# One transformer block on one core: the start of attention with the modulation as rows, gate work moved to later slots, four moves at the seams of the MLP

## The chip, the cores and the metric

One core of a Trainium2 chip runs the whole program. TensorE (PE) multiplies matrices into PSUM banks of 512 columns; VectorE (DVE), ScalarE (ACT) and GpSimd (POOL) do the elementwise work; SyncE (SP) and ScalarE issue DMAs. The metric is the device time of one execution in microseconds. The times below are the median of three executions and one profiled execution.

## The reference

```
mod = (silu(c) @ wmod).reshape(8, 6, 1, 512)      # c: 8x512, wmod: 512x3072
sa, ca, ga, sb, cb, gb = mod[:, 0..5]
ga, gb = sign(g) * maximum(|g|, 0.25)             # each gate, sign(0) = +1
h = layernorm(x) * (1 + ca) + sa                  # x: 8x512x512
x = x + ga * attention(h, W_attn, W_proj)         # 16 heads of 32, causal
h = layernorm(x) * (1 + cb) + sb
x = x + gb * mlp(h)                               # 512-1024-1024-512, relu
```

All of it is in float32; the kernel gets there with operands split into a high and a low part of reduced precision and three products of them for each matmul (TERMS).

## The kernel before

`attention` and then `mlp` run as two stages, each with its own program for each engine and with semaphores between the engines. In `attention` the eight batches are worked in a pipeline of slots: slot p handles head pair p (of 8), and has five units u. In a unit TensorE writes scores by query (`score` banks) for pair p and scores by key (`key_score` banks) for pair p-2, the weighted values of pair p-3 (`o_bank`), and some items of the list `SEQUENCE`: four TURNs (transposes of the normalised x, then modulated into `h_parts`), eight QK units of four items, eight V units of two. Items of the next batch lie in slots 4 to 7. `WORK` and `PER_SLOT` set this order by hand; every engine walks the same slots in program order. For the first batch the items of slots 4 to 7 have nothing to lie beside, so they run ahead of slot 0 (`before_first`: four TURNs, QK 0 to 3, one V unit). The names of this part, with their lines:

- `mod_columns(s)` (PE, L769) makes shift and scale as columns (512 values down the partitions, 8 batches across): 32 matmuls of 8 moving columns for a half s of the modulation (0 for attention, 1 for the MLP). `take_columns` (DVE, L619, L620) and `take_mod` (L569) read them.
- `gate_rows(g)` (PE, L776) makes a gate as 8 rows of 512: four matmuls of 512 moving columns. `take_gate` (DVE, L627 to L636) turns it into the clamped gate in five operations and SP stores it (L350).
- `wqkv_raw` is loaded in six blocks; `weights_high(k)` (ACT, L502) and `weights_low(k)` (DVE, L613) split block k. QK 0 and QK 1 need blocks 0 and 1.
- A TURN goes from PE (L725) to ACT `modulate` (`full`, L468), DVE `h_high` (L578) and POOL `low_part` (L403); QK 0 (PE, L735) waits for the low part of each quarter. `qk_hi` (ACT, L473) and `qk_lo` (DVE, L582) take a QK unit, and `load_stack(n, g)` (SP, L322) copies it with 12 DMAs into `stack[g]`, from which slots 2g and 2g+1 make their scores.
- `ones(g)` (POOL, L388) writes two rows of ones in `stack[g]`.

In `mlp` each layer is a product by seven half-size products (Strassen's form) for each of 8 batches: chunks n = 0 to 7 expand, 8 to 15 middle, 16 to 23 contract. `product(n, s)` (PE, L2149, in the last layer L2145) waits for the low part of its data operand (`lo`, DVE, L1703) and, in the first chunk of a layer, of its weights (`w2_lo` L1841, `w3_lo` L1846). `w2_sum` (L1806, L1813) makes sums of weight blocks. `second_sum` (L1727) adds up a result and has to wait until its buffer has been stored. SP's loads and stores of this stage run through one queue in program order.

## Time and profile before

| | us |
|---|---|
| median of three executions (lowest, highest) | 1541.73 (1539.03, 1541.76) |
| profiled execution | 1542.99 |
| its span from first to last instruction | 1541.2 |

The span is 1.8 us shorter than the time of the same execution; the rest lies around it. A row of the timeline gives start, duration, engine, line, what is written and read, and in brackets how long the engine was idle before it and who ended that. In rows by stretch each engine has its busy time and the count of its instructions. A TensorE record's duration includes its way through the array, so starts tell the pace better than durations; a float32 matmul of 512 columns leaves two records.

### The profile page before, as it was taken

What the parts mean: (1) busy time and instruction counts of PE and PEld (TensorE: products, weight loads), DVE (VectorE), ACT (ScalarE), POOL (GpSimd) and SP (SyncE); (2) the same over time, 40 slices, a digit from 0 to 9 for tenths busy, and PEclk for the clock granted to TensorE, in tenths of its full rate; (3) what the DMA queues carried; (4) which work ended last, traced back from release to release, by engine and by line L of the source; (5) the groups of instructions that cost most, each with busy time, mean ns of one, the idle gap of its engine ahead of it and who ended that gap; (6) DMA issues with size and microseconds to landing.
All of it is one profiled execution on the core that took longest, in us unless ns stands there. A gap on an engine that the chain in (4) does not pass through costs nothing.

```text
span 1541.2 us, 30440 instructions
## 1 busy us (share of the span) xinstructions
PE 1449.8 (94%) x12112; PEld 1314.9 (85%) x12112; DVE 1109.9 (72%) x1957; ACT 808.2 (52%) x1462; POOL 439.2 (28%) x451
## 2 busy tenths in 40 slices
PE   7989999999999999995599999998999999999998
PEld 6678878787888888874489999998999999999998
DVE  5377877777777877673577676787766666788887
ACT  3156666667666667674355555566333333353331
POOL 2146665667666766664000000000000000000000
PEclk9889999999999999997799999999999999999999
DMA  6634435244434343442434454363765556688895
GB/s 219 164 85 102 120 84 127 72 121 96 119 82 121 83 123 93 98 98 81 172 126 162 158 176 159 138 213 135 251 234 201 201 210 215 231 295 266 296 304 184
DMA packets 126590, 247.16 MB, mean 160 GB/s; under 512 B 13672, under 2 KB 36200, under 8 KB 126448
## 3 DMA queue, kind: packets, MB, share of 16 engines
q1 hardware_dynamic: 122816, 242.57, 50.5%
q10 hardware_dynamic: 3632, 2.64, 0.5%
q8 instruction: 96, 1.57, 0.4%
q14 instruction: 46, 0.38, 0.1%
HBM read 114.58 MB, written 79.72 MB: 126 GB/s over the span
## 4 chain that ended last, share of the span: by engine, by line
PE 45%; DVE 4%; ACT 2%; DMA 1%; issue 1%; SPq 0%; DVEq 0%; ACTq 0%
PE sum_b L2149 12%; PE sum_e L2149 8%; PE sum_a L2149 8%; PE aux L2089 6%; PE sum_b L2145 4%; PE sum_e L2145 3%; PE sum_a L2145 3%; PE aux L2099 1%; PE aux L2077 1%; DVE w L1841 1%; DVE op L1703 1%; DMA wproj_whole<-wproj_t 1%; ACT u_c L1443 0%; DMA y_dram<-u_c 0%; DMA blk<-y_dram 0%
## 5 line engine op out<-in xcount | busy, mean ns | idle before, releaser
L429 POOL TENSOR_TENSOR prob_lo<-prob,prob_hi 128x512 f16<-128x512 f32 x256 | 296.9, 1165 | 140.8 <-ACT prob L533 140.5
L526 ACT ACTIVATE prob_hi<-key_score 128x512 f16<-128x512 f32 x320 | 191.1, 597 | 130.6 <-PE key_score L824 128.2
L2149 PE MATMUL sum_b<-op,w 128*128 128x256 f32 x1728 | 217.9, 284 | 3.2 <-DVE p_c L1743 1.6
L735 PE MATMUL lin<-h_parts,wqkv 128*128 128x512 f32 x768 | 218.5, 408 | 1.1 <-DVE h_parts L578 1.1
L2149 PEld LDWEIGHTS sum_b<-op,w 128*128 128x128 f32 x1728 | 211.2, 192 | 5.4 <-issue 3.3
L533 ACT ACTIVATE prob<-key_score 128x512 f32<-128x512 f32 x320 | 190.7, 596 | 0.0
L697 DVE TENSOR_REDUCE row_max<-score 128x1 f32<-128x512 f32 (+2 forms) x384 | 180.4, 499 | 12.8 <-PE score L811 12.1
L735 PEld LDWEIGHTS lin<-h_parts,wqkv 128*128 128x128 f32 x768 | 143.0, 195 | 30.5 <-DVE h_parts L578 3.2
L811 PE MATMUL score<-stack 96*128 96x512 f32 (+3 forms) x512 | 155.2, 364 | 0.0
L2149 PE MATMUL sum_e<-op,w 128*128 128x256 f32 x1152 | 146.6, 284 | 3.7 <-DVE w L1841 2.3
L2149 PE MATMUL sum_a<-op,w 128*128 128x256 f32 x1152 | 145.4, 284 | 0.9 <-issue 0.9
L2149 PEld LDWEIGHTS sum_e<-op,w 128*128 128x128 f32 x1152 | 141.6, 192 | 4.6 <-DVE w L1841 2.5
L824 PE MATMUL key_score<-stack 98*128 98x512 f32 (+3 forms) x512 | 144.1, 343 | 0.0
L2149 PEld LDWEIGHTS sum_a<-op,w 128*128 128x128 f32 x1152 | 141.1, 192 | 1.8 <-issue 1.0
L844 PEld LDWEIGHTS o_bank<-v_parts,prob_hi 128*128 128x128 f16 x1280 | 100.3, 99 | 29.1 <-issue 25.7
L844 PE MATMUL o_bank<-v_parts,prob_hi 128*128 128x97 bf16 x1280 | 117.2, 212 | 5.3 <-POOL prob_lo L429 2.5
L844 PE MATMUL o_bank<-v_parts,prob_lo 128*128 128x65 bf16 x1280 | 114.3, 196 | 0.0
L745 PE MATMUL lin<-wqkv,h_parts 128*128 128x256 f32 x768 | 108.9, 284 | 0.0
L745 PEld LDWEIGHTS lin<-wqkv,h_parts 128*128 128x128 f32 x768 | 102.3, 190 | 5.1
L844 PEld LDWEIGHTS o_bank<-v_parts,prob_lo 128*128 128x128 f16 x1280 | 101.8, 100 | 0.2
L2089 PE MATMUL aux<-wproj,turned 128*128 128x512 f32 x384 | 95.3, 403 | 2.8 <-DVE turned L1600 2.8
L795 PE MATMUL score<-mask_qk,ident_bf 128*128 128x256 bf16 (+1 forms) x320 | 82.9, 259 | 13.9 <-DVE row_max L697 7.1
(153 smaller groups left out, 2577.1 us busy)
## 6 DMA issues: line engine op xcount, KB each, us to landing
stack<-qk_parts SPq DMA_DIRECT2D x384, 128.0 KB, 2.4
late_op_whole<-y_dram SPq DMA_DIRECT2D x40, 512.0 KB, 4.9
y_dram<-u_c SPq DMA_DIRECT2D x32, 512.0 KB, 3.0
blk<-y_dram SPq DMA_DIRECT2D x32, 512.0 KB, 4.1
y_dram<-y_sum SPq DMA_DIRECT2D x24, 512.0 KB, 4.4
x_tiles<-x SPq DMA_DIRECT2D x32, 256.0 KB, 3.7
attn_dram<-o_rows SPq DMA_DIRECT2D x32, 256.0 KB, 2.3
attn_tiles<-attn_dram SPq DMA_DIRECT2D x8, 1024.0 KB, 6.1
```

The lines of the kernel that those rows point to most:

```text
L429: nc.gpsimd.tensor_tensor(prob_lo[:, key[1] % 2, u, :], prob[:, u, :], prob_hi[:, key[1] % 2, u, :], ALU.subtract).then_inc(lo_pool, 1)
L526: nc.scalar.activation(prob_hi[:, q % 2, u, :], bank[:], ACT.Exp, scale=SOFTMAX_SCALE, bias=P_SHIFT)
L533: nc.scalar.activation(prob[:, u, :], bank[:], ACT.Exp, scale=SOFTMAX_SCALE, bias=P_SHIFT)\
L697: last = nc.vector.reduce_max(row_max[:, p % 2, hh, t:t + 1], bank[:, col:col + P * (t + 1)], AX.X)
L735: mm = nc.tensor.matmul(lin_bank_of((QK, f))[:], wqkv[:, wl, c, at:at + P], h[:, hl, c, :], start=(c == 0 and k == 0), stop=(c == NC_ - 1 ...
L745: mm = nc.tensor.matmul(lin_bank_of((V, g, t))[:, 0:C // 2], h[:, hl, c, t * P:(t + 1) * P], wqkv[:, wl, c, at:at + C // 2], start=(c == 0 ...
L811: mm = nc.tensor.matmul(bank[:, col:col + n], rows[:, 0, t * P:(t + 1) * P], rows[:, 1, 0:n], start=False, stop=True, skip_group_check=True)
L824: mm = nc.tensor.matmul(bank[:, col:col + n], rows[:, 1, t * P:(t + 1) * P], rows[:, 0, t * P:T], start=False, stop=True, skip_group_check ...
L844: mm = nc.tensor.matmul(o_bank[:, i * VW + low:(i + 1) * VW], part[:, p % 2, u, at:at + P], v[:, j, head, low:VW], start=(j == 0 and part ...
L2089: mm = nc.tensor.matmul(bank[:], turned[:, dl, c, t * P:(t + 1) * P], wproj[:, wl, c, :], start=(c == 0 and i == 0), stop=(c == NC_ - 1 an ...
L2145: mm = nc.tensor.matmul(dst, data[:, dl, c, cols], w3[s][:, wl, c, :], start=begin, stop=end, skip_group_check=again)
L2149: mm = nc.tensor.matmul(dst, w[:, wl, c, cols], data[:, dl, c, :], start=begin, stop=end, skip_group_check=again)
```

## The change

At the start of attention TensorE first runs 16 matmuls of the bf16 identity with itself (`warm_up`), as soon as POOL has made it. Then shift and scale are made as rows, as the gates were (`mod_row_of`, `condition_row`: four matmuls of 512 columns each), copied out by ACT (`take_row`), and turned into columns by eight small transposes (`mod_columns`). For the MLP's half this is done in slot 0 (u 1 and 3) and slot 1 (u 4), no longer ahead of slot 0; the gates' rows are made in slot 1 (u 2) and slot 2 (u 2), and their arithmetic is four operations on DVE, one to a unit, in slots 2 and 3. The four first TURNs have four banks and four buffers for themselves; QK 0 and 1 take turns by quarters; the six weight blocks are split in another order. SP loads the MLP's modulation and the first gate right behind the weights, copies `stack0` head by head, with one semaphore for each, stores the gates in slot 3, and copies `stack3`, which now shares its place with the gates, only after that. POOL makes the ones of `stack2` in slot 1 and those of `stack3` in slot 4.

In the MLP: `load_x2(1)` moves behind the stores of chunk 16's start; `w2_sum(2)` and `w2_sum(3)` go half by half to later places; `w2_lo(6)` goes ahead of three operations of chunk 8; in chunk 16 `lo(n, 4)` goes ahead of `w3_lo(5)` and `w3_lo(6)` behind `lo(n, 5)`.

TensorE's order at the start of the program, before (`lin<-ident,x_tiles` are the TURNs, `lin<-h_parts,wqkv` the QK items, `lin<-wqkv,h_parts` the V unit):

```order
L769 MATMUL o_bank<-silu,wmod_sb 128x8 x32
L725 MATMUL lin<-ident,x_tiles 128x128 x16
L735 MATMUL lin<-h_parts,wqkv 128x512 x24
L769 MATMUL o_bank<-silu,wmod_sb 128x8 x32
L735 MATMUL lin<-h_parts,wqkv 128x512 x24
L745 MATMUL lin<-wqkv,h_parts 128x256 x12
```

and now:

```order
L843 MATMUL score<-ident_bf 128x512 x16
L848 MATMUL key_score<-wmod_sb,silu 8x512 x8
L801 MATMUL lin<-ident,x_tiles 128x128 x8
L863 MATMUL o_bank<-ident,mod_rows 128x8 x8
L801 MATMUL score<-ident,x_tiles 128x128 x8
L811 MATMUL lin<-h_parts,wqkv 128x512 x48
L821 MATMUL lin<-wqkv,h_parts 128x256 x12
```

Both runs of 32 narrow matmuls are gone; the 48 QK matmuls follow each other.

VectorE's order in slot 1, from unit 0's row maximum to unit 4's (`row_max<-score` is what frees a score bank), before:

```order
L697 TENSOR_REDUCE row_max<-score 128x1
L582 TENSOR_TENSOR qk_parts<-lin,qk_parts 128x512
L559 BN_STATS bn_stats<-x_tiles 128x6
L562 BN_AGGR mean_var<-bn_stats 128x2
L697 TENSOR_REDUCE row_max<-score 128x1 x2
L559 BN_STATS bn_stats<-x_tiles 128x6
L562 BN_AGGR mean_var<-bn_stats 128x2
L627 TENSOR_SCALAR gate_sign<-key_score 8x512
L628 COPY gates<-key_score 8x512
L630 SCALAR_TENSOR_TENSOR gates<-gates 8x512
L633 TENSOR_SCALAR gates<-gates 8x512
L636 TENSOR_TENSOR gates<-gates,gate_sign 8x512
```

The same stretch now, and below it what stands in slot 3:

```order
L773 TENSOR_REDUCE row_max<-score 128x1
L650 TENSOR_TENSOR qk_parts<-lin,qk_parts 128x512
L627 BN_STATS bn_stats<-x_tiles 128x6
L630 BN_AGGR mean_var<-bn_stats 128x2
L773 TENSOR_REDUCE row_max<-score 128x1 x2
L627 BN_STATS bn_stats<-x_tiles 128x6
L630 BN_AGGR mean_var<-bn_stats 128x2
L756 TENSOR_SCALAR max_rows<-turn 8x128
```

```order
L697 TENSOR_SCALAR gate_sign<-gates 8x512
L773 TENSOR_REDUCE row_max<-score 128x1 x2
L650 TENSOR_TENSOR qk_parts<-lin,qk_parts 128x512
L642 TENSOR_SCALAR x_tiles<-x_tiles,mean_var,rstd 128x512
L701 TENSOR_TENSOR gates<-gates,gate_sign 8x512
```

The gate operations left slot 1 and lie one by one between the row maxima of slots 2 and 3.

VectorE's order at the start of chunk 16, before (`u_c<-sum_b,p_c` is `second_sum`, `late_op` a data operand's low part):

```order
L1682 TENSOR_TENSOR y_sum<-u_c,y_sum 128x1024
L1846 TENSOR_TENSOR w_5<-w_5_whole,w_5 128x1024
L1846 TENSOR_TENSOR w_6<-w_6_whole,w_6 128x1024
L1727 TENSOR_TENSOR u_c<-sum_b,p_c 128x512
L1703 TENSOR_TENSOR late_op<-late_op_whole,late_op 128x1024
L1736 TENSOR_TENSOR u_c<-sum_e,u_c 128x512
L1703 TENSOR_TENSOR late_op<-late_op_whole,late_op 128x1024
```

and now:

```order
L1790 TENSOR_TENSOR y_sum<-u_c,y_sum 128x1024
L1811 TENSOR_TENSOR late_op<-late_op_whole,late_op 128x1024
L1954 TENSOR_TENSOR w_5<-w_5_whole,w_5 128x1024
L1835 TENSOR_TENSOR u_c<-sum_b,p_c 128x512
L1844 TENSOR_TENSOR u_c<-sum_e,u_c 128x512
L1811 TENSOR_TENSOR late_op<-late_op_whole,late_op 128x1024
L1954 TENSOR_TENSOR w_6<-w_6_whole,w_6 128x1024
```

`lo(16, 4)` stands ahead of `second_sum`, and one of the two weight parts behind the operand of the next product.

The diff, cut to what sets times and order:

```diff
-        raw = Memory(nc, raw_ctx).sb("wqkv_raw", [P, NC_, 3 * C])
-    stack += [mem.sb(f"stack{g}", [P, 2, 4, T], F32R) for g in range(GROUPS // 2, GROUPS)]
+        wm_gate = raw_mem.sb("wmod_gate", [P, NC_, C])
+    stack.append(mem.sb("stack2", [P, 2, 4, T], F32R))
     with ExitStack() as gate_ctx:
+    stack.append(mem.sb("stack3", [P, 2, 4, T], F32R))
...
+    WARM_UP = 16
...
+    def turn_bank_of(n, c):
+        return score_bank[c - 2] if n == 0 and c >= 2 else lin_bank_of((TURN, c))
...
+                if n == 0 and g == 0:
+                    sp.sem_inc(stack_in[0], 16 * STACK_DMAS)
                     for j in range(4):
-                        src = f32(qk_parts[32 * j:32 * j + 32, g % 2, :, :, :]).rearrange("p s l n -> p (s l) n")
-                        step = 2 + k_part - q_part
-                        sp.dma_start(f32(stack[g][32 * block_row:32 * block_row + 32, :, j, :]),
-                                     src[:, q_part:q_part + step + 1:step, :]).then_inc(stack_in[g], 16)
+                        for block_row in range(3):
+                            load_rows(g, block_row, j, first_stack_in[j])
+                    return
+                if n == 0 and g == 3:
+                    sp.wait_ge(gates_out, 16)
+                for block_row in range(3):
+                    for j in range(4):
+                        load_rows(g, block_row, j, stack_in[g])
...
-            for step in (1, 2):
-                sp.wait_ge(mod_mm, step)
-                for half in range(2):
-                    load_mod(sp, 2 * step + half)
-                for item in before_first():
-                    if item[0] == QK and item[1] // 2 == step - 1:
-                        after_item(0, item)
+            for half in range(2):
+                sp.wait_ge(mod_mm, half + 1)
+                load_mod(sp, 2 + half)
+            load_mod(sp, 4)
+            for item in before_first():
+                after_item(0, item)
...
-                    if first and (p, u) == (1, 3):
+                    if first and (p, u) == (3, 0):
                         sp.wait_ge(gate_step, GATE_STEPS)
...
+                if first and p == 1:
+                    pool.wait_ge(w_lo, len(W_ORDER))
+                    pool.wait_ge(v_split, values_until(1))
+                    ones(2)
+                    pool.wait_ge(ones_ready, 4)
+                if first and p == 4:
+                    pool.wait_ge(mod_mm, 6)
+                    pool.wait_ge(gates_out, 16)
+                    pool.wait_ge(v_split, values_until(4))
+                    pool.wait_ge(lo_pool, 3 * len(LO_ON_POOL))
+                    ones(3)
+                    pool.wait_ge(ones_ready, 1 + GROUPS)
...
+            def take_row(s, j):
+                act.wait_ge(mod_mm, 2 * s + j + 1)
+                nc.scalar.copy(mod_rows[:, s, j], key_bank[j][0:B, :]).then_inc(mod_row, 1)
+            def take_gate(g):
+                act.wait_ge(mod_mm, 4 + g + 1)
+                act.wait_ge(w_lo, len(W_ORDER))
+                nc.scalar.copy(gates[:, g], (key_bank[0], o_bank)[g][0:B, :]).then_inc(gate_row, 1)
+            for j in range(2):
+                take_row(0, j)
+            weights_high(0)
             for item in before_first():
                 after_item(0, item, very_first=True)
+                if item == (TURN, 1):
+                    weights_high(1)
                 if item == (TURN, NC_ - 1):
+                    weights_high(2)
+                if item == (QK, 1, NC_ - 1):
                     for k in range(3, len(W_ORDER)):
                         weights_high(k)
 
             def slot(b, p, first, more):
                 if first and p == 2:
-                    act.wait_ge(gates_out, 16)
+                    act.wait_ge(mod_turned, 2)
                 for u in range(UNITS):
+                    if first and p == 0 and u in (2, 4):
+                        take_row(1, u // 2 - 1)
+                    if first and (p, u) == (1, 2):
+                        take_gate(0)
+                        load_mod(act, 5)
+                    if first and (p, u) == (2, 3):
+                        take_gate(1)
...
+            def gate_part(g, i):
+                made = 4 * g
+                if i == 0:
+                    dve.wait_ge(gate_row, g + 1)
+                    nc.vector.tensor_scalar(sign[:, g], gates[:, g], 0.0, 0.5, ALU.is_ge, ALU.subtract)\
+                        .then_inc(gate_step, 1)
+                elif i == 1:
+                    dve.wait_ge(gate_step, made + 1)
+                    nc.vector.tensor_tensor(gates[:, g], gates[:, g], sign[:, g], ALU.mult).then_inc(gate_step, 1)
+                elif i == 2:
+                    dve.wait_ge(gate_step, made + 2)
+                    nc.vector.tensor_scalar(gates[:, g], gates[:, g], GATE_FLOOR / 2, 4.0, ALU.max, ALU.mult)\
+                        .then_inc(gate_step, 1)
+                else:
+                    dve.wait_ge(gate_step, made + 3)
+                    nc.vector.tensor_tensor(gates[:, g], gates[:, g], sign[:, g], ALU.mult).then_inc(gate_step, 1)
...
-            for k in range(3):
-                weights_low(k)
             take_columns(0)
             dve.wait_ge(mod_taken, 2)
             take_mod(0)
+            weights_low(0)
             for item in before_first():
                 after_item(0, item)
-                if item == (TURN, NC_ - 1):
-                    for k in range(3, len(W_ORDER)):
-                        weights_low(k)
-            take_columns(1)
+                if item == (TURN, 1):
+                    weights_low(1)
+                if item == (QK, 1, NC_ - 1):
+                    weights_low(2)
+            weights_low(3)
...
+                    if first and p == 0 and u in (1, 3):
+                        weights_low(4 + u // 2)
+                    if first and (p, u) == (2, 0):
+                        take_columns(1)
+                    if first and p in (2, 3) and u:
+                        gate_part(p - 2, u - 1)
...
+            def warm_up():
+                for _ in range(WARM_UP):
+                    nc.tensor.matmul(score_bank[0][:], ident_bf[:], ident_bf[:].unsqueeze(1).broadcast_to([P, NT, P]),
+                                     start=True, stop=True)
+            def condition_row(bank, weights):
+                for c in range(NC_):
+                    mm = nc.tensor.matmul(bank[0:B, :], silu[:, c, :], weights[:, c, :],
+                                          start=(c == 0), stop=(c == NC_ - 1))
+                mm.then_inc(mod_mm, 1)
+            def mod_row_of(s, j):
+                pe.wait_ge(wm_in[j], 16 * (s + 1))
+                if s:
+                    pe.wait_ge(mod_row, j + 1)
+                condition_row(key_bank[j], wm[:, j])
             def mod_columns(s):
                 for j in (SHIFT, SCALE):
-                    pe.wait_ge(wm_in[j], 16 * (s + 1))
+                    pe.wait_ge(mod_row, 2 * s + j + 1)
                     for block in range(NC_):
                         at = ((s * 2 + j) * NC_ + block) * B
-                        for c in range(NC_):
-                            mm = nc.tensor.matmul(o_bank[:, at:at + B], wm[:, j, c, block * P:(block + 1) * P],
-                                                  silu[:, c, :], start=(c == 0), stop=(c == NC_ - 1))
-                mm.then_inc(mod_mm, 1)
-            def gate_rows(g):
-                pe.wait_ge(wm_in[g], 16 * 3)
-                for c in range(NC_):
-                    mm = nc.tensor.matmul(key_bank[g][0:B, :], silu[:, c, :], wm[:, g, c, :],
-                                          start=(c == 0), stop=(c == NC_ - 1))
-                mm.then_inc(mod_mm, 1)
+                        mm = nc.tensor.transpose(o_bank[:, at:at + B], mod_rows[:, s, j, block * P:(block + 1) * P],
+                                                 ident[0:B, 0:B])
+                mm.then_inc(mod_turned, 1)
+            def gate_row_of(g):
+                pe.wait_ge(wm_gate_in, 16 * (g + 1))
+                if g == 0:
+                    pe.wait_ge(mod_row, 3)
+                else:
+                    pe.wait_ge(mod_taken, 2 * MOD_STEPS)
+                condition_row((key_bank[0], o_bank)[g], wm_gate)
 
             pe.sem_inc(pv_done, PV_CREDITS)
+            pe.wait_ge(pool_step, 8)
+            warm_up()
             pe.wait_ge(silu_step, 3)
-            mod_columns(0)
-            pe.wait_ge(pool_step, 8)
-            for item in before_first():
+            for j in (SHIFT, SCALE):
+                mod_row_of(0, j)
+            first_items = before_first()
+            first_items[NC_:3 * NC_] = [item for pair in zip(qk(0), qk(1)) for item in pair]
+            for item in first_items:
                 do_item(0, item)
-                if item == (QK, 1, NC_ - 1):
-                    pe.wait_ge(mod_taken, MOD_STEPS)
-                    mod_columns(1)
+                if item == (TURN, 1):
+                    mod_columns(0)
...
+                if first and p == 6:
                     pe.wait_ge(ones_ready, 1 + GROUPS)
-                if first and p == 3:
-                    pe.wait_ge(mod_taken, 2 * MOD_STEPS)
                 for u in range(UNITS):
-                    if first and p == 0 and u in (2, 4):
-                        gate_rows(u // 2 - 1)
+                    if first and p == 0 and u in (1, 3):
+                        mod_row_of(1, u // 2)
+                    if first and (p, u) == (1, 2):
+                        gate_row_of(0)
+                    if first and (p, u) == (1, 4):
+                        mod_columns(1)
+                    if first and (p, u) == (2, 2):
+                        gate_row_of(1)
...
                     load_x2(0)
-                    load_x2(1)
@@ contract(n), k == 0
                         store_sum(n - 1, i)
+                    load_x2(1)
...
@@ expand(n), last
-                    w2_sum(3)
+                    w2_sum(2, (1,))
+                    w2_sum(3, (0,))
                 lo(n, 3)
+                if last:
+                    w2_sum(3, (1,))
...
@@ expand(n), k == B - 2
-                    w2_sum(2)
+                    w2_sum(2, (0,))
...
@@ middle(n)
                 lo(n, 4)
+                if n == B:
+                    w2_lo(6)
                 if not last:
                     first_op_sum(n + 1)
                 third_sum(n)
                 if last:
                     w3_sum(0)
                 lo(n, 5)
-                if n == B:
-                    w2_lo(6)
...
@@ contract(n)
                 lo(n, 3)
                 if first:
                     late_sums(n - 1, 1)
+                    lo(n, 4)
                     w3_lo(5)
-                    w3_lo(6)
                 second_sum(n)
-                lo(n, 4)
+                if not first:
+                    lo(n, 4)
                 third_sum(n)
                 lo(n, 5)
+                if first:
+                    w3_lo(6)
```

## Rows read from the trace of the kernel before

**Rows 1.** The page's busy times: engine, us, share of span, instructions.
```profile
PE 1449.8 (94%) x12112; PEld 1314.9 (85%) x12112; DVE 1109.9 (72%) x1957; ACT 808.2 (52%) x1462; POOL 439.2 (28%) x451
```
**Rows 2.** Waits of TensorE: waiting line, releaser, us, times, longest.
```profile
PE score L795 <- DVE row_max L697: 7.1, 7, 3.7
```
**Rows 3.** Timeline, the first 37 us: start, duration, engine, operation, idle before.
```profile
2.44 0.29 POOL L381 TENSOR_SCALAR_AFFINE_SELECT mask_kq<-mask_kq 128x128 bf16<-128x128 bf16 x1
...
8.97 13.79 PE L769 MATMUL o_bank<-silu,wmod_sb 128*128 128x8 f32 x64 [8.97 <-DMA wmod_sb<-wmod]
...
14.38 1.23 DVE L613 TENSOR_TENSOR wqkv<-wqkv_raw,wqkv 128x1024 fp32r<-128x1024 f32 x1 [0.87 <-ACT wqkv L502]
...
22.80 0.19 DVE L619 COPY mod_cols<-o_bank 128x32 f32<-128x32 f32 x1 [4.31 <-PE o_bank L769]
...
24.56 1.66 DVE L578 TENSOR_SCALAR h_parts<-lin,mod_now 128x512 fp32r<-128x512 f32 x2 [1.26 <-ACT full L468]
...
25.45 2.49 POOL L403 TENSOR_TENSOR h_parts<-full,h_parts 128x512 fp32r<-128x512 f32 x2 [13.89 <-DVE h_parts L578]
...
28.49 8.05 PE L735 MATMUL lin<-h_parts,wqkv 128*128 128x512 f32 x24 [1.10 <-DVE h_parts L578]
```
**Rows 4.** Transfers of `wmod`, all six: issues (ns), and us from issue to landing.
```profile
L257 ACTq DMA_DIRECT2D wmod_sb<-wmod x2: 525/526/528, 1.2 to 1.8; - x2
...
DMA to landing us min/median/max: 5.1/7.4/11.3
```
**Rows 5.** Stretches of 2 us: length, PE, PEld, DVE, ACT, POOL, clock, DMA, GB/s.
```profile
10.00:12.00 2.00, 2.00 (x11) 2.00 (x11) 0.75 (x5) 0.00 (x0) 1.02 (x1) 1.00 1.06 372
...
38.00:40.00 2.00, 2.00 (x21) 2.00 (x20) 0.00 (x0) 0.00 (x0) 0.00 (x0) 1.00 0.33 73
...
42.00:44.00 2.00, 2.00 (x11) 2.00 (x11) 0.00 (x0) 0.00 (x0) 0.00 (x0) 0.50 0.90 207
```
**Rows 6.** The same view by stage: QK 2 and 3, then slots 0 to 3.
```profile
46.40:53.80 7.40, 7.40 (x25) 5.93 (x26) 0.69 (x1) 0.59 (x1) 0.00 (x0) 0.72 0.90 300
...
55.30:68.70 13.40, 13.40 (x61) 6.60 (x59) 5.53 (x15) 2.38 (x6) 7.39 (x6) 1.00 0.75 190
68.70:82.70 14.00, 7.74 (x40) 5.51 (x40) 11.83 (x26) 1.38 (x3) 0.30 (x1) 0.82 0.04 10
82.70:93.70 11.00, 11.00 (x48) 8.19 (x48) 6.30 (x16) 5.73 (x11) 4.38 (x5) 0.76 0.36 81
93.70:103.90 10.20, 10.20 (x101) 9.01 (x100) 9.58 (x20) 6.42 (x14) 4.77 (x6) 1.00 0.62 141
```
**Rows 7.** Timeline of slots 0 to 2: a gate's rows, a gate operation, six QK matmuls.
```profile
58.32 3.60 PE L776 MATMUL key_score<-wmod_sb,silu 128*8 128x512 f32 x8
...
77.87 0.68 DVE L636 TENSOR_TENSOR gates<-gates,gate_sign 8x512 f32<-8x512 f32 x1
...
89.43 1.54 PE L735 MATMUL lin<-h_parts,wqkv 128*128 128x512 f32 x6
90.81 0.28 PE L795 MATMUL score<-mask_qk,ident_bf 128*128 128x256 bf16 x1
```
**Rows 8.** Timeline of POOL: the three `ones`, and the first TURN of slot 4.
```profile
57.65 5.58 POOL L388 MEMSET stack<- 2x2048 f32 x3
...
113.31 1.27 POOL L403 TENSOR_TENSOR h_parts<-full,h_parts 128x512 fp32r<-128x512 f32 x1 [2.36 <-DVE h_parts L578]
```
**Rows 9.** Timeline of chunk 8: `first_op_sum(9)`, `w2_lo(6)`, and product 5.
```profile
1065.82 1.22 DVE L1645 TENSOR_TENSOR op_sum<-blk 128x1024 f32<-128x1024 f32 x1 [1.23 <-DMA blk<-y_dram]
...
1075.18 6.02 PE L2149 MATMUL sum_e<-op,w 128*128 128x256 f32 x48 [2.30 <-DVE w L1841]
```
**Rows 10.** Timeline of chunk 16: SP's loads of `x2`, `second_sum`, and product 4.
```profile
1369.14 1.36 SPq L1316 DMA_DIRECT2D x_tiles<-x_dram x2
...
1382.37 0.69 DVE L1727 TENSOR_TENSOR u_c<-sum_b,p_c 128x512 f32<-128x512 f32 x1 [0.77 <-DMA y_dram<-u_c]
...
1384.30 4.60 PE L2145 MATMUL sum_b<-w,late_op 128*128 128x256 f32 x24 [3.58 <-DVE late_op L1703]
```

94 lines of the change are left out of this document (51 added, 43 removed).

## The prediction, made before the changed kernel was run

> **What bounds the kernel now.** I read four views. First the page: TensorE is busy for 94% of the span [rows 1], so time can be had only where its work is cut, where it waits, or where it runs below full clock. Then its waits, then the timeline of the stretches that the change touches, then busy time and granted clock by stage.
>
> The first 55.3 us are one chain. TensorE starts at 8.97, when the shift weights have landed, and makes 32 narrow matmuls (64 records) in 13.8 us [rows 3]. The clock column reads 1.00 there, but the pace tells otherwise: 11 records in 2 us, just as at a granted 0.50, while at 1.00 it is 21 [rows 5]. So this run went at 1.2 GHz. The columns are taken at 22.80, QK 0 starts at 28.49 and QK 0 and 1 take 8.05 us [rows 3]. The second 32 narrow ones follow; under them the clock falls from 1.00 to 0.50 [rows 5], and QK 2 and 3 take 7.4 us at a mean of 0.72 [rows 6]. Slot 0 starts at 55.3 and slot 4 at 103.9. In between TensorE is only 7.74 us busy in slot 1 (14.0 us), where VectorE has 11.83 us of work [rows 6]: one wait for a row maximum is 3.7 us [rows 2]. The clock is 0.82 in slot 1 and 0.76 in slot 2 [rows 6]. In the MLP, product 5 of chunk 8 waits 2.30 us for weights that wait in VectorE's order [rows 9], and product 4 of chunk 16 waits 3.58 us and then runs slowly, 4.60 us for 24 matmuls [rows 10], where 48 of the same size take 6.02 us [rows 9].
>
> **Start of attention, up to slot 0.** The warm-up can begin when POOL has made the identities, 2.7 [rows 3]. A 512-column matmul costs (90.81-89.43)/6 = 0.23 us at full clock [rows 7], 0.46 at half: 16 end between 6.4 and 10.1. I take that they end before or about 8.97 and that the clock is then full. A row of modulation is what a gate's row was, eight records in 3.60 us with the last one's way through the array, so 3.5 us [rows 7]. Shift: 8.97 to 12.4. The scale weights are the second ACT transfer, issued at 1.8; if the longest landing, 11.3 us, is its own [rows 4], they are there at 13.1: scale ends at 16.6. The copy of 8x512 on ACT is in no row; the nearest, a VectorE operation of that shape, takes 0.68 [rows 7]; I take 0.6 and put four transposes' worth of TURN work beside it. Eight small transposes: 0.1 us each at full clock, 0.2 at half [rows 5], so 0.8 to 1.6. Columns out of PSUM and into `mod_now`: three operations of 0.19 [rows 3]. `mod_now` is ready at about 19.3 (before: 23.3).
>
> Then VectorE splits weight block 0 (1.23) and makes the first quarter of h (0.81, half of 1.66), POOL its low part (1.25) [rows 3]: QK 0 starts at 22.6. The four quarters with block 1 between them end on VectorE at 24.9 and on POOL at 26.5, so the last six of the 24 QK matmuls can't start before. At full clock they end at 27.9; at half clock to begin with, as in 8.05 us for 24 [rows 3], at 30.6. Between the scale row and QK 0 TensorE has 6 us with little work, so I take the clock to have fallen: 29.8. New here is a wait: QK 2 needs the bank of QK 0, which ends only 0.6 us before QK 1, and two operations of up to 0.68 each lie between: 30.5. QK 2 and 3 at full clock 24 x 0.23 = 5.5 (7.4 before), the V unit 1.5 as before (53.8 to 55.3) [rows 6]. Slot 0 starts at 37.5: **-17.8** (best 35.4, with QK at full clock; worst 44.5, with the rows at half clock). The second narrow run is simply gone from here. SP's three early 1 MB loads stand behind the weights in its own queue and are needed only in slots 0 and 1; the copy of `stack0` can start when QK 0 and 1 are taken, at 31, and slot 0 needs only its first head.
>
> **Slots 0 to 3.** Slot 0 has two rows at 3.60 in place of two gate rows: TensorE's work is the same. VectorE gets three weight parts, 3.7 us, on top of 5.53 in 13.4 [rows 6], hidden: 0. Slot 1: 7.74 us of work, less about 0.9 for what ran at half clock, plus a gate row 3.5 and eight transposes 1.1: 11.4 instead of 14.0, **-2.6**. The waits for row maxima go with the ten gate operations; next in line is TensorE itself. Slot 2: 11.0 us, busy throughout at a clock of 0.76. Half of it at half clock would be worth 2.6; I take 2.2, and add the other gate row: 12.3, **+1.3**. VectorE has room here (6.30). Slot 3: VectorE has 9.58 us in 10.2 and gets four operations of up to 0.68, 2.4 to 2.7. Behind each stands a row maximum for which TensorE waits one bank later. Bounds: 0, if the two banks of slack take it all, and 2.1, if VectorE sets the slot; I take **+1.2**. Sum of slots: -0.1.
>
> **Slot 4.** POOL must wait for the gate store, which SP can issue only after VectorE's last gate operation in unit 4 of slot 3. Behind the wait stand `ones(3)`, 1.86 us (5.58/3), then low parts of probabilities and of V, for which ACT's modulate and through it the TURNs wait. The store's landing is in no row. POOL has 2.36 us idle before the first TURN [rows 8]. If it stands still for 1.5 to 3 us: 1.86 + 1.5 to 3 - 2.36 = 1 to 2.5, part of which POOL catches up. Bounds 0 and 2.5, value **+1.0**. SP itself stands still at the same wait through slot 3; what is behind it, the copy of `stack3`, is needed in slot 6, two slots of 10 us later.
>
> **MLP.** Chunk 8: VectorE was idle for 1.23 us before 1065.82 for a block; `w2_lo(6)` now fills it, so `w2_lo(5)`, the releaser of product 5, comes that much sooner [rows 9]: **-1.1** (bounds 0 and -2.3). The halves of `w2_sum` move 1.2 us of work from a place where VectorE waited for ACT to one where it waited for TensorE: 0 (-0.4 to +0.3). Chunk 16: product 4 was released at 1384.3 by a low part that stood behind `second_sum`; now it is ready before, and the release is the end of `second_sum`, 1382.37+0.69 = 1383.06 [rows 10]: -1.2 for certain as long as that stays. It was itself waiting 0.77 for a store; 1 MB of `x2` no longer stands ahead of that store, so up to -0.8 more, and if the gap gets short enough for the clock not to fall, 4.60 becomes about 3.0, -1.6 more. Bounds -1.2 and -3.7, against which stands that the same megabyte now delays the operands of chunk 17. Value **-2.4**.
>
> The Trainium skill (DMA: Bandwidth & Descriptors, Queues, rings and completion order) says that within one issuing engine's row of rings each DMA engine takes descriptors in ring order. By it the store would land the whole time of a megabyte sooner, and this term would be at its far bound, the total 1.3 us lower. No row before shows that store without the load ahead of it.
>
> **The sum.** -17.8 - 0.1 + 1.0 - 1.1 - 2.4 = -20.4. Against the profiled execution's own 1542.99 that is 1522.6; the median of the runs is 1.3 lower, 1541.73, and gives 1521.3.
>
> **Rivals.** (a) *The rows run at half clock.* For it: the early narrow matmuls did [rows 5], and there may be up to 2.6 us of idleness between warm-up and rows (6.4 to 8.97) and 0.7 between shift and scale. Against: the gates' rows, of the same form, ran at full pace for 3.6 us on end [rows 7]. Price: two rows twice as long, 7 us: 1528.3. Chance 0.12. (b) *What leaves slot 1 comes back in slots 2 to 4.* VectorE sets slot 3 (+0.9 more), waits in slot 2 too (+1.5), POOL's delay goes through whole (+1.5), and QK 0 and 1 bring another wait for banks (+1.5): 1526.7. For it: VectorE's 9.58 of 10.2 us. Chance 0.12. (c) *The seams don't yield*: the late operands of chunk 17 give the gain back, or `w2_lo(5)` is then released late by ACT: +3.5, 1524.8. Chance 0.08. (d) *Slower than before.* With the narrow matmuls gone the clock still doesn't rise, from the first row to the end of slot 1. The work there at full pace is 7 + 12.5 + 13.4 + 11.4 = 44 us, and twice that would give 1565. It decides from 20.4 us of such work at half clock on. For it: mean clocks of 0.72 to 0.82 in three of the stages [rows 6]. Against: each fall comes after narrow matmuls or a wait of several us, and both are taken away. Chance 0.02. (e) Nothing gained, because slots were bound elsewhere: the chain before slot 0 has nothing beside it, so I give it 0.01.
>
> The forecast keeps 0.65, with a range of its own of 1514.5 (slot 0 at 35.4, no cost in slots 3 and 4, both seams at their far bounds) to 1525. The range for 8 in 10 reaches to (a) and (b): 1514.5 to 1529. A difference under 0.2%, 3 us, can't be told from none here. Faster 0.96, same 0.01, slower 0.03.
>
> **What would show it.** The warm-up from 2.7 and rows from 8.97 with starts 0.44 (3.5/8) apart; `mod_now` at 19 to 20; QK 0 at 22 to 23; slot 0 at 35 to 38; no wait of TensorE for row maxima over 1 us in slot 1; clock 1.00 in slots 0 to 3; in slot 3 short waits for row maxima; slot 4's TURNs up to a microsecond late against the slot's start; after that the same distances as before. Product 5 of chunk 8 waits 1.1 to 1.3 us, product 4 of chunk 16 at most 2.3. Wrong it would be if the rows' starts are 0.85 apart, if slot 0 starts after 40, or if the stretch from slot 0 to slot 4 is over 51 us (before 48.6).

## The result and the profile after

| | before | changed |
|---|---|---|
| median of four executions, us | 1541.46 | 1524.26 |
| lowest and highest | 1539.03, 1541.76 | 1521.08, 1525.6 |
| profiled execution, its span | 1542.99, 1541.2 | 1523.02, 1521.2 |

The ratio is 0.9884 with a 95% interval of 0.9869 to 0.9898: 17.9 us less (15.7 to 20.2), where 20.4 were forecast. The two profiled executions lie 20.0 us apart. Why the medians lie closer together is taken up in the first experiments and at the end.

The page's busy times now, beside [rows 1]: TensorE is busy for 11 us less, VectorE, ScalarE and GpSimd are within 4 us of what they were.

```profile
PE 1438.7 (95%) x12048; PEld 1289.6 (85%) x12048; DVE 1107.0 (73%) x1955; ACT 810.9 (53%) x1468; POOL 442.7 (29%) x451
```

The timeline of TensorE up to slot 0 in the changed kernel (start, duration, line, operation, idle before), beside [rows 3]:

```profile
2.79 5.82 PE L843 MATMUL score<-ident_bf 128*128 128x512 bf16 x16 [2.79 <-POOL mask_kq L410]
8.81 3.59 PE L848 MATMUL key_score<-wmod_sb,silu 128*8 128x512 f32 x8 [0.21 <-DMA wmod_sb<-wmod]
12.99 3.60 PE L848 MATMUL key_score<-wmod_sb,silu 128*8 128x512 f32 x8 [0.58 <-DMA wmod_sb<-wmod]
...
17.54 0.66 PE L863 MATMUL o_bank<-ident,mod_rows 8*128 8x8 f32 x8
...
22.03 8.38 PE L811 MATMUL lin<-h_parts,wqkv 128*128 128x512 f32 x24 [2.80 <-POOL h_parts L432]
31.13 5.74 PE L811 MATMUL lin<-h_parts,wqkv 128*128 128x512 f32 x24 [0.72 <-DVE qk_parts L650]
...
38.14 0.23 PE L893 MATMUL score<-mask_qk,ident_bf 128*128 128x128 bf16 x1
```

A row takes 3.6 us where its 16 narrow matmuls (32 records, half of [rows 3]) took 6.9 at half pace. QK 0 and 1 take 8.4 us where QK 2 and 3, the same work, take 5.7. The view by stage shows the clock beside it (length, PE, PEld, DVE, ACT, POOL, clock, DMA, GB/s), first QK 0 and 1, then slots 0 to 3, beside [rows 6]:

```profile
22.03:30.40 8.37, 8.37 (x24) 6.30 (x24) 2.44 (x4) 2.04 (x3) 4.59 (x3) 0.66 0.74 274
...
38.14:51.56 13.42, 13.42 (x61) 6.60 (x59) 8.10 (x14) 3.54 (x8) 6.51 (x5) 1.00 0.91 220
51.56:62.25 10.69, 10.64 (x55) 6.15 (x55) 6.69 (x18) 1.96 (x4) 0.22 (x1) 1.00 0.38 119
62.25:75.64 13.39, 12.44 (x56) 7.10 (x56) 8.48 (x21) 6.33 (x12) 4.93 (x5) 1.00 0.53 126
75.64:86.89 11.25, 10.35 (x101) 9.03 (x101) 10.54 (x23) 5.81 (x13) 4.80 (x5) 1.00 0.04 9
```

The granted clock is 0.66 under QK 0 and 1, and 1.00 in the four slots; in slots 1 and 2 it had been 0.82 and 0.76. Two waits, one in slot 2 and one in slot 3, are new; they are the first two rows below. The other two are from the MLP: product 5 of chunk 8 and product 4 of chunk 16, beside [rows 9, 10].

```profile
63.76 0.50 PE L924 MATMUL key_score<-stack 98*128 98x512 f32 x1 [0.95 <-DMA stack<-max_rows]
...
78.73 0.28 PE L893 MATMUL score<-mask_qk,ident_bf 128*128 128x256 bf16 x1 [0.90 <-DVE row_max L769]
...
1057.99 6.02 PE L2263 MATMUL sum_e<-op,w 128*128 128x256 f32 x48 [0.88 <-DVE w L1949]
...
1365.17 3.11 PE L2259 MATMUL sum_b<-w,late_op 128*128 128x256 f32 x24 [1.65 <-DVE u_c L1835]
```

Product 4 no longer runs partly at half clock: 3.11 us for its 24 matmuls, before 4.60.

### The profile page after: what moved, and what is told of

Read it like the earlier page. It is cut to its first block and busy times, and to the rows that moved or that the text cites. A ratio compares the mean times of both kernels' runs of the same rounds, so it can differ in the third digit from the quotient of the medians.

```text
span 1521.2 us, 30331 instructions
## 1 busy us (share of the span) xinstructions
PE 1438.7 (95%) x12048; PEld 1289.6 (85%) x12048; DVE 1107.0 (73%) x1955; ACT 810.9 (53%) x1468; POOL 442.7 (29%) x451
## 5 line engine op out<-in xcount | busy, mean ns | idle before, releaser
L811 PE MATMUL lin<-h_parts,wqkv 128*128 128x512 f32 x768 | 214.9, 403 | 3.5 <-POOL h_parts L432 2.8
```

Of the source, the lines that this page charges most:

```text
L811: mm = nc.tensor.matmul(lin_bank_of((QK, f))[:], wqkv[:, wl, c, at:at + P], h[:, hl, c, :], start=(c == 0 and k == 0), stop=(c == NC_ - 1 ...
```

## Experiments

Each is the changed kernel with the edit shown; each was compared with the kernel before on the same chip. "First" is the changed kernel's profile above, "again" that of its second run. A "fall" is a stretch in which the granted clock is at half. All medians but the last lie within 6 us of the changed kernel's, each with an interval of 2 to 4 us either way, so the readings rest on the traces.

**The changed kernel again.** 

> The changed kernel once more, unaltered, beside the version with all the mends, and for the spread of executions. My theory of the spread: two things differ from one execution to the next, how long the clock stays at half under QK 0 and 1 (3.4 or 6.8 us, so slot 0 starts at 37.0 to 38.5) and how many isolated stretches of 3.4 us at half clock come behind the third TURNs of the batches (0 to 5). The median is then 1521 to 1525 us, the lowest and the highest of five runs about 4 us apart, and before less this one 18 to 20 us. Rival: the four runs measured at first (1521.1 to 1525.6) were typical of a constant 1524.3; then five runs lie within 2 us of it.

Measured: 1522.76 (1521.2 to 1526.3), ratio 0.9887 (0.987 to 0.9904): the same result, and the spread is 5 us. Slot 0 started at 37.18. The profiled execution was the slowest of its four, 1526.34. Batches 1 to 4, from first TURN to first TURN, in the first profile and in this one (the column behind POOL is the clock):

```profile
93.02:176.12 83.10, 78.22 (x746) 65.52 (x745) 63.86 (x148) 55.10 (x109) 55.58 (x57) 1.00 0.49 117
176.12:256.76 80.64, 78.02 (x746) 65.51 (x745) 62.90 (x148) 54.91 (x109) 52.79 (x54) 1.00 0.44 106
256.76:337.57 80.81, 78.13 (x745) 65.48 (x744) 62.84 (x147) 54.81 (x109) 52.60 (x54) 1.00 0.44 106
337.57:419.73 82.16, 79.57 (x745) 67.08 (x744) 61.93 (x147) 54.77 (x109) 52.59 (x54) 0.98 0.43 104
```

```profile
92.15:175.61 83.46, 79.60 (x746) 67.10 (x745) 63.16 (x148) 55.10 (x110) 55.67 (x57) 0.98 0.48 117
175.61:257.73 82.12, 79.52 (x745) 67.08 (x744) 61.76 (x147) 54.79 (x109) 52.70 (x54) 0.98 0.43 103
257.73:338.93 81.20, 78.16 (x745) 65.49 (x744) 62.79 (x147) 54.87 (x109) 52.67 (x54) 1.00 0.44 107
338.93:421.10 82.17, 79.54 (x746) 67.09 (x744) 61.91 (x147) 54.80 (x109) 52.64 (x54) 0.98 0.43 104
```

The same instructions take about 78.1 or 79.5 us of TensorE, at 1.00 or 0.98. Of seven batches the first profile has three at 0.98, this one five, that of the kernel before two. The fall in batch 4 of the first profile, in stretches of 2 us (the third TURN waited 1.70 us, up to 341.11):

```profile
339.00:341.00 2.00, 0.41 (x4) 0.17 (x2) 1.47 (x4) 1.57 (x3) 0.00 (x0) 1.00 0.02 4
341.00:343.00 2.00, 1.89 (x25) 1.85 (x26) 1.53 (x4) 1.35 (x3) 1.87 (x2) 0.69 0.00 0
343.00:345.00 2.00, 2.00 (x12) 1.90 (x10) 1.69 (x4) 0.93 (x3) 2.00 (x3) 0.50 0.04 8
```

TensorE has 0.41 us of work in two, then the clock is at half for some 3.4 us under full load. From batch 2 on such a batch takes about 82.2 us and not 80.7: 1.5 us for each fall. (Batch 1 takes 83.1 without a fall and 83.5 with one; why it is long is open.)

**Calm: the wait at the third TURN filled.**

```
 def do_item(n, item):
+    if n and item == (TURN, 2):
+        pe.wait_ge(turn_taken, PAIRS * (n - 1) + NEXT_FROM + 1)
+        for _ in range(KEEP):        # 6
+            nc.tensor.matmul(turn_bank[:], ident_bf[:], ...)
```

> The changed kernel with six more matmuls of the bf16 identity (512 columns each, 1.3 us at full clock) ahead of the third TURN of batches 1 to 7, where TensorE waits 1.7 to 2.7 us for VectorE anyway; they write the bank of the turned row maxima, behind a wait that is met long before. My theory: the isolated stretches of 3.4 us at half clock during attention (three in the changed kernel's profile, five in the profile of the version with the old MLP, none in that of the version with the bridge) all begin 3 to 4 us after a batch's first TURN, so that wait is what brings them, and their number per execution is what makes executions of one kernel differ by 4 us. Filled, none is left: up to 1.7 us for each that goes, 3 to 5 us in the mean, and the runs lie closer together. Rival: the falls come from elsewhere (the many small matmuls of the weighted values); then they stay, and the time is the same or, where the six are in the way, up to 0.5 us per batch, 3.5 us, longer.

Measured: 1518.48 (1516.88 to 1519.71), ratio 0.9854 (0.9831 to 0.9877). The seven waits at the third TURN came to 13.0 us in the changed kernel; the first row is what they come to here, and the clock is 1.00 over 600 us:

```profile
PE lin L802 <- DVE h_parts L647: 3.9, 7, 1.3
```

```profile
90.00:690.00 600.00, 585.25 (x5584) 485.12 (x5582) 458.64 (x1073) 412.84 (x814) 397.52 (x400) 1.00 0.42 102
```

The theory held as far as two profiles can show it. With the six matmuls there is no fall in batches 1 to 7, here and in the version with five mends below; of the eleven profiles of the changed kernel and its variants without them, ten have one to five, and one has none. The median is 4.3 us under the changed kernel's second run. The price is small: from the third TURN of batch 1 to that of batch 7 it took 485.4 us here, and 484.6 in the one profile without fillers that had no fall. (The falls of the first batch, under QK 0 and 1 and in slot 2, remained.)

**Bridge: the wait ahead of QK 0 filled.**

```
                 if item == (TURN, 1):
                     mod_columns(0)
+                if item == (TURN, NC_ - 1):
+                    warm_up(BRIDGE, key_bank[0])    # 10
```

> The changed kernel with ten more matmuls of the bf16 identity, 512 columns each, between the last TURN and QK 0, into a bank that nothing needs there. They fill 2.3 of the 2.8 us in which TensorE waits for the first quarter of h. My theory: the granted clock fell to half at about 20.9 because TensorE had little work from 16.5 on, and that is what makes QK 0 and 1 take 8.4 us. With them the clock stays at full, QK 0 and 1 are then bound by POOL's last low part (26.6) plus six matmuls (1.4) and end at 28.0 and not 30.4: 2.4 us earlier, and slot 0 starts at 35.7. Rival: the clock falls all the same, since the stretch before (the eight small transposes and the gaps around them) is what counts; then QK 0 starts up to 2 us later, because the ten run at half pace in front of it, and the kernel is 0 to 2 us slower.

Measured: 1518.5 (1515.87 to 1519.91), ratio 0.9854 (0.983 to 0.9878). In its profile the clock is 1.00 throughout the start, and the 24 matmuls of QK 0 and 1 end at 28.7; slot 0 is at 36.41:

```profile
19.16 2.32 PE L844 MATMUL key_score<-ident_bf 128*128 128x512 bf16 x10
22.13 0.93 PE L812 MATMUL lin<-h_parts,wqkv 128*128 128x512 f32 x3 [0.65 <-issue]
23.26 5.42 PE L812 MATMUL lin<-h_parts,wqkv 128*128 128x512 f32 x21 [0.19 <-DVE wqkv L682]
```

The theory held for the clock. For the time it gave less than its 2.4 us: slot 0 starts 1.7 us sooner than in first, 0.8 sooner than in again. This execution also happened to have no fall in batches 1 to 7, which the bridge can't cause; so its total says less than its start.

**Cold: no warm-up.** `WARM_UP = 0`.

> The changed kernel without its 16 warming matmuls; nothing else differs. My theory: they are what puts the two modulation rows at full clock, so without them the starts within the shift row lie 0.85 us apart and the row takes 7 us in place of 3.6; whether the scale row is slow too depends on when the clock rises. The columns are ready 3.5 to 7 us later (shift row done at about 16, not 12.5), slot 0 starts at 41.6 to 45 (38.1 with the warm-up), and the time is 3.5 to 7 us longer, if the later waits of the start don't swallow a part. Rival: the rows would have run at full clock anyway, or the weights of the scale row (landing at 13.0) hide the slow shift row: no difference within 1 us. Which it is shows in the spacing of the eight records of each row.

Measured: 1527.57 (1526.36 to 1528.95), ratio 0.9915 (0.9892 to 0.9938). Both rows together run from 9.00 to 18.9 (8.81 to 16.6 with the warm-up), and slot 0 is at 39.64:

```profile
9.00 9.90 PE L848 MATMUL key_score<-wmod_sb,silu 128*8 128x512 f32 x16 [9.00 <-DMA wmod_sb<-wmod]
```

```profile
9.00:11.00 2.00, 2.00 (x3) 0.36 (x4) 1.24 (x6) 0.00 (x0) 0.38 (x1) 1.00 1.06 375
13.00:15.00 2.00, 2.00 (x4) 0.36 (x3) 0.60 (x2) 0.00 (x0) 0.00 (x0) 1.00 1.10 349
15.00:17.00 2.00, 2.00 (x6) 0.36 (x4) 0.00 (x0) 0.57 (x1) 0.00 (x0) 1.00 1.10 348
```

Three records in 2 us at first, then four, then six: the shift row is slow, the scale row soon isn't. The warm-up is needed, but it is worth 2.3 us at the rows and 1.5 to 2.5 at slot 0, below the 3.5 that I gave as the least. (The clock column reads 1.00 here too while the pace is half, as in [rows 5].) The median is 3.3 to 4.8 us above the changed kernel's, and in the profile the rest lies elsewhere: in chunk 8 `second_sum` waited 5.31 us for a store, where the other profiles have 3.4 to 3.5, product 5 waited 2.77 us instead of 0.88, the clock fell behind it, and the first six products took 41.29 us instead of 37.93. Whether that goes with the missing warm-up or with this execution isn't shown:

```profile
1062.39 7.50 PE L2263 MATMUL sum_e<-op,w 128*128 128x256 f32 x48 [2.77 <-DVE w L1949]
```

**QK 0 and 1 one after the other.** The line that interleaves them is taken out.

> The changed kernel with QK 0 and QK 1 one after the other, four quarters each, as in the kernel before, and not by turns. My theory: by turns, TensorE has 24 matmuls to do while POOL makes the low parts of four quarters, and only the last six wait for the last of them (26.6). One after the other, QK 0 advances at POOL's pace (one low part in 1.25 us, six records in 1.4) and ends at about 28, and QK 1's twelve follow at full pace: the end of both is at 30.8 against 30.4, 0 to 1 us later. In return QK 2's bank is free at once, and the wait of 0.72 us before QK 2 goes. In all within 0.7 us of the changed kernel. Rival: the turns are worth the 2.8 us by which twelve matmuls follow the last low part in place of six: slot 0 starts at least 1.4 us later and the time is 1.4 us longer.

Measured: 1523.57 (1520.5 to 1527.28), ratio 0.9892 (0.9867 to 0.9917). Slot 0 is at 38.93, with 6.8 us of half clock as in the first profile of the changed kernel, 38.14: the turns are worth 0.8 us. The wait before QK 2 is gone as expected. The first theory gave at most 0.7, its rival at least 1.4.

**The second gate's load behind the small copies.**

```
                         take_gate(0)
-                        load_mod(act, 5)
 ...                                  # after the two copies of max_rows
+                        if first and p == 1:
+                            load_mod(act, 5)
```

> The changed kernel with one DMA moved: ACT issues the load of the second gate's weights (1 MB) behind the two small copies of the row maxima into stack0, and not ahead of them. Queue theory: in the changed kernel the small copies stood behind that megabyte in ACT's queue, which is why slot 2 begins with a wait of 0.95 us for stack0 that the kernel before did not have; with the load behind them the wait is gone, slot 2 takes 12.4 us and not 13.4, and the time is 1.0 us shorter. Rival: the wait comes from the copies being issued late, because ACT first takes gate 0's row (58.2 to 58.8) and slot 1 has become shorter; then the load's place does nothing and the wait stays at 0.9 us within 0.2.

Measured: 1520.96 (1517.95 to 1522.29), ratio 0.9866 (0.9844 to 0.9888). ScalarE's queue in the changed kernel, then here:

```profile
58.23 0.38 ACTq L267 DMA_DIRECT2D wmod_gate<-wmod  x1
58.65 1.91 ACTq L609 DMA_DIRECT2D stack<-max_rows  x2
```

```profile
58.54 1.89 ACTq L608 DMA_DIRECT2D stack<-max_rows  x2
60.47 0.45 ACTq L267 DMA_DIRECT2D wmod_gate<-wmod  x1
```

TensorE's wait for them is gone, and slot 2 takes 12.20 us, where it took 13.39. It did so in two ways. Without the megabyte's issue ahead the copies are issued 0.45 us earlier against slot 2's start (58.54 for 62.60, and 58.65 for 62.25). And they land at most 2.6 us after the end of their issue (60.43, used without a wait at 63.01), where it was 3.2 (60.56, 63.76). The Trainium skill (DMA: Bandwidth & Descriptors, Queues, rings and completion order) says that descriptors in one ring are taken in order; the second difference agrees with it.

**VectorE's gate operations earlier.**

```
+    GATE_AT = {(1, 4): ((0, 0),), (2, 0): ((0, 1),), (2, 1): ((0, 2),), (2, 2): ((0, 3),),
+               (2, 4): ((1, 0), (1, 1)), (3, 0): ((1, 2),), (3, 1): ((1, 3),)}
```

> The changed kernel with VectorE's eight gate operations up to a slot earlier: gate 0's in unit 4 of slot 1 and units 0 to 2 of slot 2, gate 1's in unit 4 of slot 2 (two of them) and units 0 and 1 of slot 3. My theory: slot 3 was 1.05 us longer than before (11.25 against 10.2) because VectorE had 10.5 us of work in it, and slot 4's TURNs came 1.2 us later because POOL waited for the gates' store. With the store issued about 6 us earlier POOL waits for nothing: the distance from slot 4's start to its third TURN goes from 10.6 back to about 9.4, and slot 3 gets back 0.3 to 0.9 us. In all 1.3 to 2.1 us faster. Rival: slot 4's delay is POOL's own work (the memset of ones, 1.86 us, lies ahead of the low parts whatever it waits for); then the third TURN stays at 10.6 and only slot 3 gains, up to 0.9; and the operations can cost in slot 2 what they free in slot 3: no change.

Measured: 1522.56 (1521.22 to 1525.66), ratio 0.9884 (0.9862 to 0.9906): no gain. From slot 4's start to its third TURN it is 9.63 us, near the 9.4 of my theory, but slot 3 became 1.3 us longer, 12.55 us. From slot 3's start to slot 4's third TURN it is 22.2 us, in the changed kernel 21.9 (before 19.6): the time only moved from one slot to the other. And the theory's cause is overturned by this run and by the changed kernel's own trace. GpSimd doesn't wait for the gates' store; it was idle for 0.20 us before the `ones` in both. The changed kernel's row:

```profile
90.84 1.80 POOL L417 MEMSET stack<- 2x2048 f32 x1 [0.20 <-POOL v_parts L440]
```

VectorE's gate operations at the end of slot 2 here, and GpSimd's beside them, show something else: they take 1.41 and 1.52 us, where the same forms take 0.40 and 0.67 in other units.

```profile
76.47 2.46 POOL L474 TENSOR_TENSOR prob_lo<-prob,prob_hi 128x512 f16<-128x512 f32 x2 [0.30 <-ACT prob L603]
...
76.50 1.41 DVE L699 TENSOR_SCALAR gate_sign<-gates 8x512 f32<-8x512 f32 x1
77.94 1.52 DVE L703 TENSOR_TENSOR gates<-gates,gate_sign 8x512 f32<-8x512 f32 x1
```

**The products apart from GpSimd's operations.** The same table with gate 0's parts at (2,1), (2,3), (2,4), (3,1) and gate 1's at (3,1) to (3,4).

> The changed kernel with the same eight gate operations on VectorE, of which the four products of gates and sign are placed where GpSimd is idle: gate 0's at unit 3 of slot 2 and unit 1 of slot 3, gate 1's at units 2 and 4 of slot 3 (in the changed kernel units 2 and 4 of both slots). Contention theory: in the changed kernel the same product took 0.67 us while GpSimd was idle but 1.44 and 1.68 us where a GpSimd operation had begun up to 0.3 us before it (67.64 and 76.36), so VectorE, with two operands in SBUF, waited for GpSimd's operation to end; the second one is what makes TensorE wait 0.90 us for a row maximum in slot 3. Set apart, all four take 0.67 us, the row maximum comes about 1.2 us earlier, the wait is gone and slot 3 takes 10.4 us and not 11.25: 0.9 us faster. Load theory: slot 3 is long because VectorE has 10.5 us of work in it, whatever the order; then the four take 0.67 but the wait only moves to a later unit, and slot 3 stays at 11.2 within 0.2.

Measured: 1521.5 (1518.32 to 1521.98), ratio 0.9852 (0.9831 to 0.9873). A product in the changed kernel with GpSimd's operations beside it, and below it the clamp that now stands in its place:

```profile
76.36 2.78 POOL L472 TENSOR_TENSOR prob_lo<-prob,prob_hi 128x512 f16<-128x512 f32 x2 [0.30 <-ACT prob L601]
...
76.39 1.68 DVE L708 TENSOR_TENSOR gates<-gates,gate_sign 8x512 f32<-8x512 f32 x1
```

```profile
75.66 2.46 POOL L474 TENSOR_TENSOR prob_lo<-prob,prob_hi 128x512 f16<-128x512 f32 x2 [0.30 <-ACT prob L603]
...
75.68 1.42 DVE L706 TENSOR_SCALAR gates<-gates 8x512 f32<-8x512 f32 x1
...
78.68 0.67 DVE L710 TENSOR_TENSOR gates<-gates,gate_sign 8x512 f32<-8x512 f32 x1
```

All four products take 0.67 us, as the contention theory says. But the clamp, with one operand, takes 1.42 us where it stands behind a GpSimd operation and 0.41 elsewhere; the theory was too narrow. Slot 3 takes 10.98 us (wait 0.63), where the contention theory said 10.4 and the load theory 11.0 to 11.4.

**MLP as before; x2 early; order of chunk 16 back.** The first replaces the whole stage. The second moves one line, the third four:

```
                 if last:
                     load_x2(0)
+                    load_x2(1)
 ...
                         store_sum(n - 1, i)
-                    load_x2(1)
```

```
-                    lo(n, 4)
                     w3_lo(5)
+                    w3_lo(6)
                 second_sum(n)
-                if not first:
-                    lo(n, 4)
+                lo(n, 4)
```

> The changed kernel with the MLP stage exactly as in the kernel before, so only the start of attention is changed. My theory, from the two traces: the stretch from product 0 of chunk 8 to the end is 4.2 us longer than in the changed kernel (1.4 at product 5 of chunk 8, 3.4 at product 4 of chunk 16, less 0.6 of small waits in chunk 17), so the time is 4.2 us longer and the start of attention alone is worth 15.8 us against before. Rival: the gain at the seams depends on when the stores land and a good part of it is chance of the execution; then the changed kernel is only 1 to 2 us faster than this one, and before less this one is 16 us. The waits of product 5 of chunk 8 and product 4 of chunk 16 are to read 2.3 and 3.6 us again.

> The changed kernel with one move undone: the second megabyte of x2 is loaded ahead of chunk 16's stores again, and not behind them. Theory of queue order: the store for which second_sum waits lands about 0.8 us later again (the 0.77 us that VectorE waited for it before), product 4 of chunk 16 waits 2.4 us and not 1.65, and the time is 0.8 us longer; if that wait is long enough for the clock to fall, product 4 takes 4.6 us instead of 3.1 and the time is 2.3 us longer. Rival: the load costs nothing where it stood, because the transfers share the DMA engines whatever their order, and what helped in chunk 16 is only VectorE's order: the wait of product 4 stays at 1.65 us and the small waits of chunk 17 (0.16 to 0.2 us each, 0.6 in all) vanish: up to 0.6 us faster.

> The changed kernel with only VectorE's order at the start of chunk 16 as before: the low part of product 4's operand again behind second_sum, both weight parts ahead of it; the load of the second megabyte of x2 stays behind the stores. Order theory: VectorE's order did all the work in chunk 16, so product 4 waits about 2.7 us again (as in the version with the whole old MLP), the clock falls, its 24 matmuls take up to 4.6 us, and the chunk's first six products take 2.2 us longer: 1.9 us slower in all. Queue theory: with the megabyte out of the way the store lands earlier than where both moves are undone, second_sum doesn't wait for it at all, and product 4 waits 1.9 us or less (0.8 less than 2.7).

All in us; the last column is from product 0 of chunk 16 to the eleventh product:

| | median, ratio (interval) | chunk 8, first six products | chunk 16, product 4 waits | ten products from chunk 16 on |
|---|---|---|---|---|
| before | | 39.34 | 3.58 | 34.09 |
| changed, again | 0.9887 (0.987, 0.9904) | 37.93, 37.97 | 1.65, 1.66 | 31.35, 31.37 |
| MLP as before | 1524.36, 0.9888 (0.986, 0.9916) | 39.41 | 2.73 | 33.23 |
| x2 early | 1522.1, 0.9879 (0.9855, 0.9903) | 38.03 | 1.64 | 31.34 |
| order back | 1521.88, 0.986 (0.984, 0.988) | 37.95 | 2.72 | 33.05 |

Product 4 of chunk 16 in the version with the old MLP, and in the one with the order put back:

```profile
1367.12 4.60 PE L2253 MATMUL sum_b<-w,late_op 128*128 128x256 f32 x24 [2.73 <-DVE late_op L1811]
```

```profile
1361.97 4.42 PE L2256 MATMUL sum_b<-w,late_op 128*128 128x256 f32 x24 [2.72 <-DVE late_op L1811]
```

VectorE's order does all of it: with x2 early nothing changes, with the order back everything is as in the old MLP whether x2 is late or not. The wait for the store in [rows 10] (0.77) is in neither, and in no other profile of the fourteen. So with the old MLP product 5 waits 2.36 us, as expected (2.3), but product 4 waits 2.73 and not 3.6. Against the old MLP the two seams are worth 1.5 + 1.9 = 3.4 us in the traces, where I expected 4.2; the totals, with intervals of some 4 us either way, can't confirm it.

**Five mends together.** Calm, bridge, the load later, the gate operations at (2,1), (2,3), (3,1) twice, (3,2) twice, (3,3), (3,4), and `ones(3)` in slot 5 (`if first and p == 5`).

> The changed kernel with five mends together: ten bridging matmuls ahead of QK 0, six ahead of the third TURN of batches 1 to 7, the second gate's weights loaded behind the copies of the row maxima, the gate operations of VectorE in GpSimd's pauses (none at unit 4 of slot 2, which in the first try still met a GpSimd operation: 1.42 us for one of 0.41), and the ones of stack3 written in slot 5 and not in slot 4. If the mends are independent: slot 0 at 36.4 (37.0 to 38.4), slot 2 at 12.2 us (13.4), slot 3 at 10.4 (11.25), from slot 4's start to its third TURN 9.4 (10.6), no stretch at half clock in batches 1 to 7: 1.7 + 1.1 + 0.9 + 1.2 + about 4 = 9 us under the changed kernel, 1513 us on the median where that has 1522. Rival: the mends of one chain hide each other, because slots 2 to 4 are then bound by VectorE's or GpSimd's whole work: slot 3 stays over 10.8 or the 1.8 us of ones come back in slot 5, and with the bridge's gain already partly in the calm: only 5 to 6 us, 1517.

Measured: 1514.67 (1513.23 to 1516.23), ratio 0.9831 (0.9817 to 0.9846). Beside the changed kernel on the same chip, 1522.76, it is 8.1 us faster, nearer the 9 of independent mends than the 5 to 6 of the rival, and the spread is 3 us. Slot 0 is at 36.43, slot 2 takes 12.18 us, and the record has no stretch at half clock up to 690 us. Slot 3 takes 11.05 (changed 11.25): all eight gate operations run at 0.41 and 0.67, and the slot is hardly shorter. One reason is that the collision moved to another VectorE operation, which takes about 0.54 us alone; the kernel before had it there too (1.50 us at 95.67):

```profile
73.50 2.45 POOL L477 TENSOR_TENSOR prob_lo<-prob,prob_hi 128x512 f16<-128x512 f32 x2 [0.30 <-ACT prob L605]
...
74.72 1.51 DVE L648 TENSOR_SCALAR x_tiles<-x_tiles,mean_var,rstd 128x512 f32<-128x512 f32 x1
```

So the slot has such a collision in every version (with the gates early it has two, 1.41 and 1.52 us), and VectorE is busy for 10.86 of its 11.05 us: there the rival is right, VectorE's load sets it. And with the `ones` gone from slot 4, TURN 0 to third TURN is still 4.31 us (4.50; before 3.57): the memset was at most 0.2 to 0.3 us of it.

## Why the prediction was right, and where not

| step | forecast | first profile, again |
|---|---|---|
| start of slot 0 (before 55.31) | -17.8 | -17.2, -18.1 |
| slots 0 to 3 (before 48.60) | -0.1 | +0.15, +0.2 |
| slot 4 to its third TURN (before 9.37) | +1.0 | +1.3, +1.3 |
| chunk 8 | -1.1 | -1.4, -1.4 |
| chunks 16, 17 | -2.4 | -2.7, -2.7 |
| sum | -20.4 | -19.9, -20.7 |

*Start.* Rows 0.43 us apart, `mod_now` at 18.7 (19.3), QK 0 at 22.03 (22.6), its end at 30.4 (29.8), slot 0 at 38.14 (37.5). That the clock falls between the scale row and QK 0 was put into the sum, and the bridge shows it: without the fall the end is 28.7 (27.9 forecast). Rival (a), rows at half clock, did not occur: the warm-up prevents it. The cold kernel shows that the mechanism is real but that it was priced three times too high, at 7 us for 2.3: the pace doubles within the rows.

*Slots.* Slot 0 as forecast. Slot 1 took 10.7 (11.4), slot 2 13.4 (12.3), slot 3 11.25 (11.4). That the four sum to within 0.3 us of the forecast is luck: 0.7 too much in slot 1 (of which 0.5 is that the eight transposes take 0.6 us and not 1.1) nearly cancels 1.1 too little in slot 2. The excess of slot 2 is one wait of 0.95 us that I had not priced: I followed SP's and GpSimd's moved DMAs, but not ScalarE's, where the gate's megabyte had come to stand ahead of two small copies. With it moved away slot 2 takes 12.2.

*Slot 3.* The size was right (+1.07 for +1.2), the cause as put: VectorE's load. The product that met GpSimd isn't a cost on top: the kernel before had a collision of the same size in this slot, and with all eight gate operations in pauses it is back at that place, so the slot gave back only 0.2.

*Slot 4.* Right size, wrong cause, so this term is right by luck. The step said that GpSimd stands still for the gates' store. It doesn't (0.20 us idle), and without the `ones` there most of the delay stays. What the traces show is a delay that starts in slot 3. From that slot's start to slot 4's third TURN it is 19.6 us before, 21.9 in both profiles of the changed kernel, and 21.6 to 22.2 in the three versions with the gate operations elsewhere. The 2.3 us can be read off in three places; no run tests them one by one:

```profile
100.03 1.31 ACTq L541 DMA_DIRECT2D stack<-max_rows  x2
```

```profile
83.60 1.32 ACTq L609 DMA_DIRECT2D stack<-max_rows  x2
...
95.19 1.55 DVE L779 TENSOR_TENSOR prob_lo<-prob,prob_hi 128x512 f16<-128x512 f32 x1
```

ScalarE's copies of the row maxima, for which VectorE has to be done, are issued 7.96 us after slot 3's start, before 6.30 (the first row): 1.7 us, with the gate operations ahead on VectorE. The V parts follow on ScalarE; one of them then waits 0.89 us for VectorE instead of 0.49: 0.4. And VectorE's `prob_lo`, ahead of the operand that frees the third TURN's bank, began 0.16 us behind a GpSimd operation and took 1.55 us instead of 0.67, which makes the TURN 0.3 us later. That last part is gone where the `ones` are moved to slot 5.

*Seams.* Chunk 8 within its bounds. In chunk 16 product 4's wait is 1.9 us shorter than before, and its 24 matmuls 1.5 faster; 0.7 of new small waits stand behind it. Of the 1.9 the order gave 1.1, as the term's certain part had it; the other 0.8, the wait for the store, is absent with the old MLP too (2.73 for 3.58), so x2 didn't bring it: that part of the term is luck of the execution. The rule on ring order of the Trainium skill (DMA: Bandwidth & Descriptors, Queues, rings and completion order), by which the total would have been 1.3 us lower, is not refuted by this, it had nothing to act on.

*The rest of the span.* The table leaves out three stretches, and in the first profile they happen to sum to 0. From the third TURN of batch 1 to that of batch 7 it is 488.7 us before, 489.6 and 492.1 in the two profiles of the changed kernel; from there to the MLP's first product 1.2 and 0.8 us less than before; and chunk 7, where the halves of `w2_sum` went, is 0.3 and 1.45 us longer (forecast -0.4 to +0.3; 0 to 1.4 in the variants). So the second profile is only 16.7 us under that of before, though its steps sum to 20.7.

*The median.* By steps the gain is 20 us, by the two ratios 17.9 and 17.4. A part of the gap is the falls in batches 1 to 7, about 1.5 us each: two in the profile of before, three and five in those of the changed kernel. In the nine experiments without the calm the count goes from 0 to 4 with no trend, so nothing says that the change brings them; how often they come in before was seen in one profile only, so the gap between 20 and 17.5 stays partly open.

## What to carry to other kernels

Here a wait of TensorE of about 2 us could cost twice, once itself and once by the half clock after it, and not in every execution: look for such waits where runs of one kernel spread, and try filling them with matmuls into a free bank. When a DMA is moved, look what small, urgent transfer is issued behind it in the same engine's queue, on every engine. When an operation is moved off a collision, look which one takes its place. And a forecast of the right size can stand on the wrong cause: read the idle time of the engine that is said to wait.

## What the runs showed of the hardware

VectorE and GpSimd hold each other up. Over the fourteen traces, each of the 22 gate operations of VectorE that began 0.03 to 0.26 us behind a GpSimd operation took 1.41 to 1.68 us instead of 0.40 to 0.67, the products of two operands as well as comparisons and clamps of one. The 15 that began first, with a GpSimd operation behind them, took 0.67 or 0.68, and the GpSimd operation then took 1.33 to 1.67 us instead of 1.16. The same product shows both: 1.44 us at 67.89 in the changed kernel, 0.25 us behind GpSimd, and in the version with x2 early, where it came 0.05 us ahead:

```profile
67.92 0.67 DVE L701 TENSOR_TENSOR gates<-gates,gate_sign 8x512 f32<-8x512 f32 x1
67.97 1.64 POOL L472 TENSOR_TENSOR prob_lo<-prob,prob_hi 128x512 f16<-128x512 f32 x1 [2.46 <-ACT prob L601]
```

The Trainium skill (SBUF — State Buffer, SBUF: two separate sides) says that they share a pair of ports as an exclusive lock, for a VectorE operation in a fast mode, or with two SBUF inputs against a GpSimd operation that reads SBUF. The durations agree: the rest of the GpSimd operation plus the operation's time alone gives 1.14 + 0.67 = 1.81 for the measured 1.68, 0.90 + 0.67 = 1.57 for 1.44, and 1.14 + 0.41 = 1.55 for 1.42, each 0.13 us too much.

TensorE's clock fell from 2.4 to 1.2 GHz behind a wait of 1.7 us in some batches and not in others with the same wait. With six matmuls in the wait it stayed at 2.4 GHz in all seven.
